# Two products of an attention and expert-mixing kernel moved from the vector engine to ScalarE copies and GpSimd, with the bias on x added earlier

## What is computed

```python
xn = layernorm(x)
q  = (xn @ Wq + bq)                       # 16 heads of 8
lat = xn @ Wl + bl
k, v = lat @ Wk + bk, lat @ Wv + bv
attn = softmax(q @ k.T / sqrt(8)) @ v @ Wo + bo
# experts: 8 heads, queries of 32 split in halves of 16, batch-normed, l2-normed
s0, s1 = q0 @ k0.T, q1 @ k1.T             # 32 scores each
ts0, ts1 = top_k(s0, 4), top_k(s1, 4)     # 16 combinations, index = ti0 * 32 + ti1
w  = softmax(ts0[:, None] + ts1[None, :])
out = sum_k up[idx_k] * w_k * gelu(down[idx_k] . xn)
return x + attn + out
```

## Time and profile before

| | |
|---|---|
| median of 3 runs | 362.45 us (361.98 to 363.92) |
| the profiled execution | 363.47 us, its span 361.6 us |
| PE busy | 322.1 us, 89% |
| DVE busy | 329.7 us, 91% |
| ACT busy | 253.2 us, 70% |
| POOL busy | 249.4 us, 69% |
| mean granted TensorE clock | 0.976 of full speed |

### The profile page before, as it was taken

How to read it: one execution, slowest core, us unless ns; L and a number is a source line. 1 busy time by engine, 2 the same in 40 slices (tenths; PEclk the granted TensorE clock), 3 DMA queues, 4 the chain that set the end, 5 groups by cost and what they waited for, 6 DMA issues and landing times.

```text
span 361.6 us, 9653 instructions
## 1 busy us (share of the span) xinstructions
PE 322.1 (89%) x3080; PEld 174.4 (48%) x3080; DVE 329.7 (91%) x1421; ACT 253.2 (70%) x388; POOL 249.4 (69%) x531
## 2 busy tenths in 40 slices
PE   3998898966997979999999999999999999999886
PEld 2454553332453445455455554554545455455545
DVE  6599989899897888999999999999999999999972
ACT  3699977976674755767767667767686767767681
POOL 6388882438698695677777686967777777777820
PEclk9999999995898999999999999999999999999999
DMA  4765666248231406060404233142504060000101
GB/s 122 201 173 141 180 167 162 60 81 97 61 32 33 58 5 102 4 104 17 89 20 90 56 50 73 33 84 25 95 11 105 5 104 18 3 18 3 32 3 29
DMA packets 45887, 24.82 MB, mean 69 GB/s; under 512 B 5452, under 2 KB 45708, under 8 KB 45836
## 3 DMA queue, kind: packets, MB, share of 16 engines
q1 hardware_dynamic: 45836, 24.20, 32.0%
HBM read 15.54 MB, written 8.39 MB: 66 GB/s over the span
## 4 chain that ended last, share of the span: by engine, by line
DVE 46%; PE 22%; POOL 13%; issue 12%; ACT 5%; POOLq 0%; DVEq 0%; ACTq 0%
DVE negm L973 21%; DVE r_sb L1031 7%; DVE top L1011 7%; POOL prod L1261 4%; PE bank L664 3%; PE bank L690 3%; PE SJ L746 2%; PE SI L603 2%; PE bank L683 2%; DVE r_sb L1045 1%; POOL x_sb L1176 1%; PE bank L620 1%; ACT fqT L323 1%; DVE fst L896 1%; PE SI L526 1%
## 5 line engine op out<-in xcount | busy, mean ns | idle before, releaser
L973 DVE TENSOR_REDUCE negm<-SI 128x4 f32<-128x1024 f32 x128 | 154.1, 1214 | 4.9 <-PE SI L603 4.8
L431 ACT ACTIVATE Eb<-SJ 128x1024 f32<-128x1024 f32 x117 | 119.4, 1020 | 29.9 <-PE SJ L644 29.8
L664 PE MATMUL bank<-Eb,vhat 128*18 128x256 f32 x1024 | 71.3, 398 | 0.9 <-ACT Osb L462 0.9
L1261 POOL TENSOR_TENSOR prod<-r_sb,a 128x1024 f32<-128x1024 f32 x28 | 53.5, 1912 | 16.5 <-issue 16.4
L603 PE MATMUL SI<-KS,QS 48*128 48x256 bf16 x512 | 51.1, 279 | 7.1 <-DVE negm L973 7.1
L644 PE MATMUL SJ<-QS,KS 50*128 50x256 bf16 x484 | 48.8, 281 | 7.0 <-ACT Eb L431 6.9
L1011 DVE MAX8 top<-s_sb 128x8 f32<-128x32 f32 x480 | 47.4, 177 | 2.9 <-ACT s_sb L398 2.8
L1031 DVE MATCH_REPLACE8 r_sb<-top,s_sb 128x36 f32<-128x36 f32 x240 | 40.4, 180 | 0.0
L603 PEld LDWEIGHTS SI<-KS,QS 48*128 48x128 bf16 x512 | 18.2, 95 | 44.6 <-issue 33.4
L664 PEld LDWEIGHTS bank<-Eb,vhat 128*18 128x18 f32 x1024 | 24.6, 99 | 28.4 <-issue 15.8
L690 PE MATMUL bank<-cst,prod 128*128 128x128 f32 x240 | 32.4, 278 | 3.3 <-ACT s_sb L398 2.8
(11 more groups left out here) (212 smaller groups left out, 611.6 us busy)
## 6 DMA issues: line engine op xcount, KB each, us to landing
qk_parts<-parts SPq DMA_DIRECT2D x48, 128.0 KB, 2.4
QS<-qk_parts SPq DMA_DIRECT2D x32, 96.0 KB
KS<-qk_parts SPq DMA_DIRECT2D x32, 96.0 KB
x_sb<-L_attn_x SPq DMA_DIRECT2D x8, 256.0 KB, 3.5
QS<-qk_parts SPq DMA_DIRECT2D x32, 64.0 KB
KS<-qk_parts SPq DMA_DIRECT2D x32, 64.0 KB
out<-ysb SPq DMA_DIRECT2D x16, 128.0 KB, 3.2
QS<-qk_parts SPq DMA_DIRECT2D x32, 32.0 KB
```

Of the source, the lines that this page charges most:

```text
L431: A(Eb[:, n % 4, :], SJ[:, :], ACT.Exp).then_inc(s["ex"], 1)
L664: last = mm(psO[32 * c:32 * c + 2 * VC, (q % 2) * S:(q % 2 + 1) * S], vhat[:, v0:v0 + 2 * VC], Eb[:, (2 * g + c // 2) % 4, e0:e0 + S], sta ...
L973: V.tensor_reduce(negm[:, bb % 2, :, :, pr].rearrange("p t e -> p e t"), SI[slot % 2][:, :].rearrange("p (e t j) -> p e t j", e=2, j=S), a ...
L1261: TT(prod[:, t, :, :, :], r_sb[:, hs, 0:NK].unsqueeze(2).to_broadcast([P, FH, TOP, NK]), a0[:, hs, :].unsqueeze(3).to_broadcast([P, FH, TO ...
```

## The change

1. The gating product wgT: ScalarE copies the turned products out of PSUM (k = 5), GpSimd multiplies them with gT. `turn_outputs` waits for the copy, `finish` for the product.
2. The heads: ScalarE copies the turned outputs out of PSUM into `heads` (288 elements per partition, in the memory of `fwq_in`), VectorE takes the reciprocal at the end of slot 5, GpSimd multiplies. `turn_heads` moves from k = 6 to k = 7, behind `sj`.
3. The copies of the best four move from GpSimd to ScalarE, one after the exponential of k = 3 and one after that of k = 4.
4. Two scalings into z_sb become one instruction.
5. The bias on x is added in the last round of the prologue (three quarters) and at slot 8 (the fourth).
6. The replacements are spread 4, 6, 2, 4 over k = 4 to 7.
7. GpSimd splits the maxima before it works out the gate coefficients, which move from k = 6 to k = 7.

The last sequence, whose work stands after the loop, keeps its products on VectorE.

```diff
@@ act
+            def best_four(b, t):
+                hs = slice(FH * t, FH * (t + 1))
+                act.wait_ge(s["t8"], 2 * b + t + 1)
+                if b >= 1:
+                    act.wait_ge(s["mr"], 4 * b)
+                A(top4[:, hs, 0:TOP], top8[:, hs, 1, 0:TOP], ACT.Copy).then_inc(s["t4"], 1)
...
+                bw = (slot - LAG - 10) // 8
+                if k == 5 and 0 <= bw < B:
+                    act.wait_ge(s["wt"], 2 * (bw + 1))
+                    if bw >= 1:
+                        act.wait_ge(s["y"], bw)
+                    A(wgT[:, :], psM[:, 0:S], ACT.Copy).then_inc(s["wt_ev"], 1)
...
+                if k in (3, 4) and 0 <= b < B:
+                    best_four(b, k - 3)
+                if k == 5 and 0 <= bw < B:
+                    act.wait_ge(s["ct"], bw + 1)
+                    if bw >= 1:
+                        act.wait_ge(s["on"], bw)
+                    A(heads, psM.rearrange("p (c r) -> p c r", r=32)[:, :, 0:2 * VC].rearrange("p c (u v) -> p c u v", u=2),
+                      ACT.Copy).then_inc(s["ct_ev"], 1)
@@ pe
-                if b < LB:
-                    pe.wait_ge(s["wg"], b + 1)
+                if b < LB - 1:
+                    pe.wait_ge(s["wt_ev"], b + 1)
+                elif b == LB - 1:
+                    pe.wait_ge(s["wg"], LB)
...
                 pe.wait_ge(s["onT"], b + 1)
+                pe.wait_ge(s["wg"], b + 1)
...
+                b = (slot - LAG - 12) // 8
+                if k == 7 and 0 <= b < B:
+                    turn_heads(b, psM)
...
-                b = (slot - LAG - 11) // 8
-                if k == 6 and 0 <= b < B:
-                    turn_heads(b, psM)
@@ dve
-                    for h in range(NH // 4 * quarter, NH // 4 * (quarter + 1)):
+                    for h in range(REPLACED[quarter], REPLACED[quarter + 1]):
...
-                b = (slot - LAG - 9) // 8
-                if k == 4 and 0 <= b < B:
-                    dve.wait_ge(s["wt"], 2 * (b + 1))
-                    dve.wait_ge(s["g_ev"], NC)
+                b = (slot - LAG - 10) // 8
+                if k == 5 and 0 <= b < B:
+
+                    dve.wait_ge(s["ct_ev"], b + 1)
                     if b >= 1:
-                        dve.wait_ge(s["y"], b)
-                    V.tensor_tensor(wgT[:, :], psM[:, 0:S], gT[:, b * S:(b + 1) * S], ALU.mult).then_inc(s["wg"], 1)
+                        dve.wait_ge(s["on"], b)
+                    V.reciprocal(rden[:, :].rearrange("p (c u) -> p c u", u=2), heads[:, :, :, DH]).then_inc(s["rd"], 1)
@@ pool
+            def biased(i):
+                part = slice(i * NT // 4, (i + 1) * NT // 4)
+                TT(x_sb[:, part, :], x_sb[:, part, :], bo_sb[:, :].unsqueeze(1).to_broadcast([P, NT // 4, D]), ALU.add)\
+                    .then_inc(s["xb"], 1)
...
+                if c == NC - 1:
+                    biased(0)
+                    biased(1)
...
+            def gated(b):
+                pool.wait_ge(s["wt_ev"], b + 1)
+                if b == 0:
+                    pool.wait_ge(s["g_ev"], NC)
+                TT(wgT[:, :], wgT[:, :], gT[:, b * S:(b + 1) * S], ALU.mult).then_inc(s["wg"], 1)
+
+            def normalised(b):
+                pool.wait_ge(s["rd"], b + 1)
+                pool.wait_ge(s["ct_ev"], b + 1)
+                if b >= 1:
+                    pool.wait_ge(s["onp"], b)
...
+                    if b >= 1:
+                        gated(b - 1)
+                        normalised(b - 1)
                     pool.wait_ge(s["cmp"], 2 * b + 1)
```

More of the change, by code:

```diff
@@ L98, in program @@
         wo_sb = sb("wo_sb", [P, D])
-        fwq_sb = sb("fwq_sb", [P, 2 * P]); down_sb = sb("down_sb", [P, D]); up_sb = sb("up_sb", [P, D])
+        fwq_in = sb("fwq_in", [P, BT * H * VC]); down_sb = sb("down_sb", [P, D]); up_sb = sb("up_sb", [P, D])
+        fwq_sb = fwq_in[:, 0:2 * P]
+        heads = fwq_in[:, :].rearrange("p (c u v) -> p c u v", u=2, v=VC)
         downT = sb("downT", [P, E])
@@ L171, in program @@
         FILTER = 2
-        BIAS_SLOTS = (8, 9, 21, 29)
+        REPLACED = (0, 4, 10, 12, 16)
         names = (
@@ L975, in _ @@
                                     axis=AX, op=ALU.max, negate=True).then_inc(s["mx"], 1)
[L976 to L987, removed]
                 b = slot // 8 - 1
@@ L1153, in residues @@
                 TT(parts[:, c % 2, 1, 2, :], r32[:, 1, :], parts[:, c % 2, 1, 1, :], ALU.subtract).then_inc(s["lo_k"], 1)
+                if c == NC - 1:
+                    biased(2)
             for c in range(NC):
@@ L1169, in _ @@
                     last.then_inc(s["krep"], 1)
+            def gated(b):
[8 more added lines that the diff above has]
+                    pool.wait_ge(s["onp"], b)
+                TT(on[:, :, :].rearrange("p t (c u v) -> p (t c) u v", u=2, v=DH), heads[:, :, :, 0:DH],
+                   rden[:, :].rearrange("p (c u) -> p c u", u=2).unsqueeze(3).to_broadcast([P, BT * H // 2, 2, DH]),
+                   ALU.mult).then_inc(s["on"], 1)
             for slot in range(NSLOT):
@@ L1172, in _ @@
                 b = slot // 8 - 1
-                if slot in BIAS_SLOTS:
-                    i = BIAS_SLOTS.index(slot)
-                    part = slice(i * NT // 4, (i + 1) * NT // 4)
-                    TT(x_sb[:, part, :], x_sb[:, part, :], bo_sb[:, :].unsqueeze(1).to_broadcast([P, NT // 4, D]), ALU.add)\
-                        .then_inc(s["xb"], 1)
-                if k in (2, 3) and 0 <= b < B:
-                    t = k - 2
-                    hs = slice(FH * t, FH * (t + 1))
-                    pool.wait_ge(s["t8"], 2 * b + t + 1)
-                    if b >= 1:
-                        pool.wait_ge(s["mr"], 4 * b)
-                    V.tensor_copy(top4[:, hs, 0:TOP], top8[:, hs, 1, 0:TOP]).then_inc(s["t4"], 1)
+                if slot == 8:
+                    biased(3)
                 if k == 3 and 0 <= b < B:
+                    pool.wait_ge(s["t8"], 2 * b + 2)
                     pool.wait_ge(s["fs_ev"], 2 * b + 2)
@@ L1223, in _ @@
                     V.tensor_scalar(rank[:, 1, :, :], rank[:, 0, :, :], float(TOP), None, ALU.is_lt).then_inc(s["sel"], 1)
-                if k == 6 and 0 <= b < B:
+                bm = slot // 8
+                if k == 7 and bm < B:
+                    pool.wait_ge(s["mx"], NPAIR * (bm + 1))
+                    if bm >= 1:
+                        pool.wait_ge(s["mt"], bm)
+                    most = negm[:, bm % 2, :, :, :]
+                    V.tensor_copy(mpart[:, :, :, 0, :], most).then_inc(s["mh"], 1)
+                    pool.wait_ge(s["mh"], bm + 1)
+                    TT(mpart[:, :, :, 1, :], most, mpart[:, :, :, 0, :], ALU.subtract).then_inc(s["ms"], 1)
+                if k == 7 and 0 <= b < B:
                     pool.wait_ge(s["ze"], b + 1)
@@ L1241, in _ @@
                     TT(p0r[:, 2, :], p0r[:, 1, :], dinv[:, :, 0], ALU.mult).then_inc(s["rest"], 1)
-                bm = slot // 8
-                if k == 7 and bm < B:
-                    pool.wait_ge(s["mx"], NPAIR * (bm + 1))
-                    if bm >= 1:
-                        pool.wait_ge(s["mt"], bm)
-                    most = negm[:, bm % 2, :, :, :]
-                    V.tensor_copy(mpart[:, :, :, 0, :], most).then_inc(s["mh"], 1)
-                    pool.wait_ge(s["mh"], bm + 1)
-                    TT(mpart[:, :, :, 1, :], most, mpart[:, :, :, 0, :], ALU.subtract).then_inc(s["ms"], 1)
                 b = slot // 8 - 2
@@ L1295, in _ @@
             TT(z_sb[:, :, NK:NK + TOP], s_last[:, :, 0, 0:TOP], each(0, TOP), ALU.mult)
-            TT(z_sb[:, :, NK + TOP:NK + 2 * TOP], top8[:, :, 0, 0:TOP], each(0, TOP), ALU.mult)
-            TT(z_sb[:, :, NK + 2 * TOP:ZW], top8[:, :, 1, 0:TOP], each(1, TOP), ALU.mult)
+            TT(z_sb[:, :, NK + TOP:ZW].rearrange("p h (a k) -> p h a k", a=2), top8[:, :, :, 0:TOP],
+               rb.unsqueeze(3).to_broadcast([P, NH, 2, TOP]), ALU.mult)
             TT(z_sb[:, :, 0:NK], s_last[:, :, 1, 0:NK], each(1, NK), ALU.mult).then_inc(s["z"], 1)
```

10 lines of the change are left out of this document (7 added, 3 removed), and 2 rows, old and new, of the table names.

## The result

The changed kernel takes 358.21 us (median of 4 runs, 357.70 to 358.51); the kernel before, run beside it, 362.22 us (4 runs, 361.91 to 363.92). The ratio is 0.9878, 95% interval 0.9845 to 0.9912. The profiled execution took 357.70 us, with a span of 355.9 us.

What follows compares the result with a forecast made beforehand. It put the weight on the ACT and PE path in slots 5 to 7, with full DVE worth at most 0.41 us a cycle. -7.0 + 1.2 + 0.6 = -5.2 us from 362.45 gave 357.2 us, range 352.0 to 360.5.

Steps and rivals of the forecast that it cites:

- The bias cycles: Two long cycles with bias additions become ordinary ones, 20.45 to 16.95 us each: -7.0 us.
- stretch and stall go together: Behind PE's stall at L675 (2.12 us), the slow stretch (1.38 us) goes too; were it to stay, only 4.2 us would go.
- ACT and PE, slots 5 to 7: Heads' longer handoff from ACT to PE fills SI's old wait and adds 0.1 us in each of 12 cycles: +1.2 us.
- The last cycle: No SI in slot 7 to fill, so finish comes 1.33 us after SJ instead of 0.65: +0.6 us.
- DVE: Sheds two products and short waits, some 0.9 us a cycle; PE's 0.41 us wait in slot 7 goes.
- POOL: Gains two products of 0.64 us, busy 13.4 us a cycle; products and mpart stay in time for PE: all hidden.
- The prologue: Bias additions moved into holes of POOL's queue, low parts 0.5 us later but covered: cost 0, otherwise 0.5 us once.
- DVE's relief reaches the cycle: Rival: added handoffs are hidden and 0.41 us comes back in 12 cycles, 4.9 us: 350.6 us, chance 0.2.
- The third rival: POOL is late, PE waits for the heads' product and mpart: slower than before, 368 us with 2 us products; chance 0.07.

Runs made afterwards that it cites:

- second profile of before: The kernel before, run once more with no edit for another profile: 360.86 us, span 359.0 us.
- second profile of after: The changed kernel, run once more with no edit for another profile: 358.57 us, span 356.8 us.
- first group's runs: The kernel before with no edit, run beside the first four experiment kernels: 361.8 us median of 11 runs.

## Why the prediction was right, and where it was off

The forecast was 357.2 us in a range of 352.0 to 360.5; measured were 358.21 us. The mechanism was the forecast one.

- *The bias cycles.* They became ordinary ones, as said. The term of -7.0 us was mis-sized: it was read from one execution in which both stalls had a slow stretch behind them, and taken off the median of the runs, which the prediction itself had 1.02 us below that execution. Beside its own runs the edit alone gave 5.0 us; the second profile of before shows one stall without the stretch, and only three of 33 runs had the clock of the first. The stalls of 1.9 to 2.1 us came all four times that the two profiles show the additions of slots 21 and 29, the 1.4 us behind them three times of four. The sentence on which this hung, "I take it that stretch and stall go together", is the step that failed. The Trainium skill (TensorE: Matmul & The Clock Gate, What's actually happening) says that the array runs at half rate until activity releases it. The trace agrees (granted clock 0.50 from 84 to 92 us, 1.00 from 94 on, in the first profile), but that does not tell whether a given stall has a slow stretch behind it: of two stalls of 1.88 us one had and one had not.
- *ACT and PE, slots 5 to 7.* Forecast +0.1 us a cycle, measured +0.09 in most of the ordinary cycles and +0.08 as the mean of all 13 against those of the kernel with the bias edit alone (221.50 and 220.47 us in all). Step by step, from the exponential of slot 5: the next exponential was forecast 1.96 us on (211.04 to 213.00) and came at 1.89, SJ of slot 7 3.04 and 2.97, the turn of the heads 3.36 and 3.30, `finish` 4.37 and 4.30. The copy of the heads took 0.41 us (estimate 0.40). The gate's copy ahead of the exponential of slot 5 was hidden, as forecast: from SJ to that exponential it is 0.43 us (219.33 to 219.76) and was 0.44 (210.65 to 211.09).
- *The last cycle.* Forecast +0.6; the second profile of after has a last part of 32.84 us against 32.25 in the second of before and 32.24 in the first, +0.6. The kernel with the heads back on VectorE has 32.24 and the one with the bias edit alone 32.28, so it is the heads' handoff.
- *DVE.* Its relief was forecast to be lost but for the 0.41 us wait that the handoff fills. That held. Both products of 0.425 us left its queue, but its busy time, in which overlapping instructions count once, fell by 0.54 us and not by 0.85 or 0.9.
- *POOL.* The products took 0.74 and 0.63 us (estimate 0.64; what makes the first longer was not tested), mpart was ready at 226.37 and PE's matmul on it came at 227.23, 0.9 us later. Hidden, as forecast. Busy time rose to 14.1 us, forecast 13.4: the coefficients lie beside L1063 now, and the first of them took 0.78 us, where it had taken 0.32 (L1228, median). In one cycle it was mpart that lay there:

```profile
209.21 0.69 DVE L1063 SCALAR_TENSOR_TENSOR r_sb<-r_sb,z_sb 128x512 f32<-128x512 f32 x1
209.22 0.78 POOL L1269 TENSOR_TENSOR mpart<-negm,mpart 128x32 bf16<-128x32 f32 x1
...
210.20 0.29 PE L698 MATMUL bank<-cst,mpart 128*32 128x128 bf16 x2
...
226.24 0.69 DVE L1063 SCALAR_TENSOR_TENSOR r_sb<-r_sb,z_sb 128x512 f32<-128x512 f32 x1
226.32 0.78 POOL L1274 TENSOR_TENSOR p<-rank,z_sb 128x64 f32<-128x64 f32 x1
```

The rule of the Trainium skill (GPSIMD Engine Reference, Key points) that the prediction weighed, contention of POOL with VectorE's instructions that have two SBUF inputs, is borne out: in this trace one of 14 mpart splits took 0.78 us, the one beside L1063, against a median of 0.25, and in that cycle the coefficient L1274 took 0.31. The prediction expected this for the coefficients, off PE's path; that it can reach mpart, which is on it, it did not see.

- *The prologue.* Forecast cost 0. POOL adds 4.68 us ahead of the low parts (59.57 to 64.20). From the product in front of them (L1149 before, at 57.77 us; L1172 after, at 57.35) to the first SJ (79.70 and 79.27) it is 21.93 and 21.92 us, and 21.92 or 21.93 in nine of the ten other profiles, with the additions there or not: hidden. The 0.4 us between 79.27 and 79.70 were there before the additions and are none of their doing. (The tenth has 23.39 and a granted clock of 0.70 from 62 to 66 us.)
- *The rivals.* The first (DVE's relief reaches the cycle, 350.6 us) did not come, but it was close at hand: with the gate's half of the relief alone, and edits 3, 4 and 7, which were not run by themselves, the cycles are 16.68 us. The prediction summed up the relief of the two products as one term; the runs show that the handoff of the second, as it is queued here, takes back what the relief gives. The third rival, POOL late, had 0.9 us to spare in most cycles, but 0.2 in the one above (mpart ready at 210.00, PE's matmul at 210.20), and came true for one cycle in the kernel with the gate back on VectorE.

The sum by measured terms: -5.0 for the bias (first group's runs), +1.0 for the 13 cycles (+0.08 each), +0.6 at the end, which gives -3.4; measured were -4.0 (358.21 against 362.22), with an interval of 3.2 to 5.6 us. The difference of 0.6 is within what such runs can tell.

## What to carry to other kernels

When an engine is full and another waits for it, list for each piece of work that could leave it what the *handoff* is queued behind on the receiving engine: here a copy of 0.41 us ahead of an exponential that PE waits for took back all that two products less on VectorE could give, while a copy of 0.38 us in a gap of the same queue was free. When a wait is removed and nothing is gained, look at the next instruction on the same path: two limits in series show no gain one by one and 0.37 us a cycle together. And a loss read from a single execution should be split into the stall and the clock behind it, since the second may not come in the next execution.

## What the runs showed of the hardware

- Two idle gaps of PE of 1.88 us each, at the same place of the program in the same execution: behind one the granted clock stayed at 1.00 (values of 16 matmuls in 1.06 us), behind the other it fell (scores in 0.59 us instead of 0.38, clock over the cycle 0.92). In another execution a gap of 2.04 us was followed by values in 1.91 us.
- A stretch at the lower level also came without any such gap in one execution of two of the same kernel: ahead of 334.28 us PE had waited 0.66 and 0.87 us, and had the same two waits in the execution in which the clock stayed at 1.00.
- Each of these stretches moved an execution by 1.4 to 1.5 us. The timed runs of one kernel beside each other spread by 0.8 to 3.4 us, and their mean granted clocks fall into steps with the time: 0.976, 0.980 to 0.981 and 0.985 for the kernel before, with medians of 363.65, 362.76 and 360.78 us. Where in each timed run the stretches lay is not on record.
- A POOL instruction beside DVE's SCALAR_TENSOR_TENSOR with two SBUF inputs (0.68 to 0.69 us) takes longer: mpart 0.76 to 0.78 us instead of 0.25, L1274 0.78 instead of 0.31, L1236 0.81 instead of 0.23.
